# Attention values product turned round: probabilities as weights, values and ones as the moving side

## The reference, cut to what matters

```
Q = x @ wq (+ bq);  K = c @ wk (+ bk);  V = c @ wv (+ bv)      # c is x or the context
scores = Q K^T / sqrt(dk);  scores = where(mask == 0, -big, scores)
A = softmax(scores, axis=-1)
out = A @ V, heads side by side;   out @ wo (+ bo)
```

## Time and profile before

| | |
|---|---|
| median of 3 executions | 726.18 us (725.76 to 728.63) |
| profiled execution, its own time | 727.51 us |
| profiled execution, span from first to last instruction | 725.6 us |
| busy: PE / PE weight loads / DVE / ACT / POOL | 659.6 / 468.9 / 509.8 / 455.5 / 319.8 us |
| mean granted TensorE clock | 0.956 of full |

### The profile page before, as it was taken

How to read it: one execution, slowest core, us unless ns; L and a number is a source line. 1 busy time by engine, 2 the same in 40 slices (tenths; PEclk the granted TensorE clock), 3 DMA queues, 4 the chain that set the end, 5 groups by cost and what they waited for, 6 DMA issues and landing times.

```text
span 725.6 us, 26905 instructions
## 1 busy us (share of the span) xinstructions
PE 659.6 (91%) x9470; PEld 468.9 (65%) x9470; DVE 509.8 (70%) x1259; ACT 455.5 (63%) x1274; POOL 319.8 (44%) x540
## 2 busy tenths in 40 slices
PE   1999999999999999999999779899946989999995
PEld 1566666777777766666666537899933656666773
DVE  0598999888887778888888633344413689988784
ACT  1467677777777787777777442355513567777874
POOL 2244544466667653333477661245532254543110
PEclk9999999999999999999999669999975899999998
DMA  8333434332333321111111001122232011111110
GB/s 265 92 100 91 95 94 95 75 71 66 97 90 112 89 69 34 44 36 42 37 53 39 25 32 45 31 65 68 64 108 70 23 35 43 35 29 33 48 41 27
DMA packets 60047, 47.32 MB, mean 65 GB/s; under 512 B 7833, under 2 KB 54429, under 8 KB 58800
## 3 DMA queue, kind: packets, MB, share of 16 engines
q1 hardware_dynamic: 53152, 28.57, 14.2%
q10 hardware_dynamic: 4528, 13.25, 7.4%
q0 software_dynamic: 2272, 4.24, 1.8%
HBM read 25.41 MB, written 14.79 MB: 55 GB/s over the span
## 4 chain that ended last, share of the span: by engine, by line
PE 68%; issue 15%; POOL 7%; DVE 4%; ACT 2%; DMA 2%; ACTq 1%; SPq 0%; POOLq 0%; DVEq 0%
PE ps L569 11%; PE ps L606 9%; PE ps L792 5%; PE ps L730 5%; PE ps L803 5%; PE ps L655 4%; PE ps L643 4%; PE ps L672 4%; PE ps L738 4%; POOL k_by_j L499 3%; PE ps L711 3%; PE ps L758 2%; PE ps L656 2%; PE ps L591 2%; PE ps L683 2%
## 5 line engine op out<-in xcount | busy, mean ns | idle before, releaser
L1098 DVE TENSOR_REDUCE top<-ps 128x16 f32<-128x1024 f32 (+1 forms) x96 | 108.9, 1134 | 38.7 <-PE ps L569 37.0
L499 POOL TENSOR_TENSOR k_by_j<-k_t,cst 128x512 f32<-128x512 f32 (+1 forms) x96 | 95.6, 996 | 81.4 <-ACT k_t L907 45.0
L491 POOL TENSOR_TENSOR rstd<-spread,half_neg 128x1 f32<-128x1 f32 x80 | 44.6, 557 | 193.2 <-DVE spread L1191 115.0
L569 PE MATMUL ps<-k_by_j,q_t 32*64 32x256 f32 (+1 forms) x1536 | 123.8, 392 | 1.2
L606 PE MATMUL ps<-cst,prob 128*128 128x128 f32 x704 | 119.7, 291 | 1.7 <-ACT prob L928 1.5
L606 PEld LDWEIGHTS ps<-cst,prob 128*128 128x128 f32 x704 | 76.8, 143 | 61.5 <-issue 45.2
L1057 DVE RECIPROCAL inv<-ps 128x128 f32<-128x128 f32 x96 | 91.8, 956 | 32.9 <-PE ps L738 30.6
L928 ACT ACTIVATE prob<-prob 128x1024 f32<-128x1024 f32 (+1 forms) x96 | 94.8, 988 | 22.8 <-DVE prob L1114 22.5
L1114 DVE TENSOR_TENSOR prob<-ps,top 128x1024 f32<-128x1024 f32 (+1 forms) x96 | 108.3, 1128 | 0.7
L877 ACT ACTIVATE prob_t<-ps 128x512 f32<-128x512 f32 (+1 forms) x96 | 53.9, 561 | 38.0 <-PE ps L606 37.5
L865 ACT ACTIVATE prob_t<-ps 128x512 f32<-128x512 f32 (+1 forms) x96 | 53.9, 561 | 28.5 <-PE ps L606 27.4
(11 more groups left out here) (155 smaller groups left out, 1213.4 us busy)
## 6 DMA issues: line engine op xcount, KB each, us to landing
sorted_rows<-zero_rows ACTq DMA_DIRECT2D x32, 276.2 KB, 2.7
stage_m<-in_m SPq DMA_DIRECT2D x80, 64.0 KB, 2.0
stage_x<-x_t SPq DMA_DIRECT2D x80, 64.0 KB, 1.9
mow<-in_mow SPq DMA_DIRECT2D x18, 256.0 KB, 3.1
stage_kv<-in_ctx_t SPq DMA_DIRECT2D x64, 64.0 KB
rows_in<-sorted_rows SPq DMA_DIRECT2D x39, 65.0 KB, 1.8
wat<-in_wat ACTq DMA_DIRECT2D x1, 1280.0 KB, 7.6
stage_x<-in_x_t SPq DMA_DIRECT2D x16, 64.0 KB, 2.0
```

What stands on the lines that cost most here:

```text
L499: pool.tensor_tensor(k_by_j[:, p, 0:nj, :], k_t[:, p:p + 1, :].broadcast_to([128, nj, TOK]), cst[:, cj:cj + nj].unsqueeze(2).broadcast_to( ...
L569: mm = pe.matmul(ps[S * b:S * b + S, 2 * p + bank, r * nj * S:(r + 1) * nj * S].rearrange("p (h k) -> p h k", k=S), q_t[rows_g, p, S * b:S ...
L1098: dve.tensor_reduce(top[:, p, 0:nh].rearrange("p (b h) -> p b h", b=2), sc, AX.X, ALU.max).then_inc(top_d, 1)
```

## The change

The values product is turned round. The transposed probabilities (128 rows, 64 queries as columns) are now the stationary weights, and the values are the moving side. The moving side has, for a pair of heads, the values of both heads and two columns that are one on the rows of the even or the odd head: 18 columns for heads of 8 features, 34 for heads of 16. So the product gives values and sums at once, and the eight matmuls (L738) with ones as weights are gone. There are no zero columns any more, and nothing is accumulated. The result has tokens on the partitions, `heads_q`; DVE takes the reciprocal of 16 (or 8) sums a token instead of 128, and multiplies with a broadcast. Because the output projection needs features on the partitions, PE transposes `heads_q` (new, in the slot ahead of the transpose of the normalised rows), and ACT copies that from PSUM into `heads_t` (new, between the copy of the second half of the probabilities and the copy into `x_t`). The output projection waits for this copy (`ht_e`) instead of for DVE. ACT copies the values in two instructions a pair instead of four in the phases with 16 heads. GpSimd writes the two columns of ones once, at the start.

```
-        v_16 = sb("v_16", [128, 2, 2, 8, 32])
-        v_8 = sb("v_8", [128, 2, 2, 4, 32])
+        v_16 = sb("v_16", [128, 2, 2, 8, 18])
+        v_8 = sb("v_8", [128, 2, 2, 4, 34])
-        inv = sb("inv", [128, 2, D])
+        inv = sb("inv", [128, 2, 16])
+        heads_q = sb("heads_q", [128, 2, D])
...
+        def heads_at(pair):
+            nh = heads(pair)
+            w = 2 * D // nh + 2
+            at_ = ps[:, B_HEADS, 0:nh // 2 * w].rearrange("p (q c) -> p q c", c=w)
+            return at_[:, :, 0:w - 2], at_[:, :, w - 2:w]
...
@@ pool, once @@
+            for vb, w in ((v_16, 18), (v_8, 34)):
+                q = vb.shape[3]
+                pool.tensor_copy(vb[:, :, :, :, w - 2:w].rearrange("p a b q c -> p (a b q) c"),
+                                 cst[:, C_HALF:C_HALF + 2].unsqueeze(1).broadcast_to([128, 4 * q, 2])).then_inc(set_ones, 1)
...
@@ pe, slot, ahead of the transpose of the normalised rows @@
+                pr = at(OFF_OUT)
+                if pr is not None:
+                    wait_pair(pe, heads_d, pr)
+                    pe.transpose(ps[:, B_HEADS, HT], heads_q[:, pr.p, :], ident).then_inc(ht_d, 1)
...
@@ pe, output projection @@
-                    wait_pair(pe, heads_d, pr)
+                    wait_pair(pe, ht_e, pr)
...
@@ pe, values product @@
-                    wait_pair(pe, heads_d, pr, 1)
+                    wait_pair(pe, ht_e, pr, 1)
...
-                    for b in range(2):
-                        for k in range(step):
-                            for g in range(4):
-                                q = g * step + k
-                                half, c = divmod(q, npr // 2)
-                                mm = pe.matmul(ps[32 * g:32 * g + 32, B_HEADS, S * b:S * b + S],
-                                               vb[:, p, b, q, :],
-                                               prob_t[:, p, half, c * 128 + S * b:c * 128 + S * b + S],
-                                               start=k == 0, stop=k == step - 1, skip_group_check=True)
-                    for k in range(step):
-                        for g in range(4):
-                            half, c = divmod(g * step + k, npr // 2)
-                            mm = pe.matmul(ps[32 * g:32 * g + 32, B_HEADS, 128:128 + TOK], own_ones(pr, k),
-                                           prob_t[:, p, half, c * 128:c * 128 + TOK],
-                                           start=k == 0, stop=k == step - 1, skip_group_check=True)
+                    for q in range(npr):
+                        half, c = divmod(q, npr // 2)
+                        for b in range(2):
+                            mm = pe.matmul(ps[S * b:S * b + S, B_HEADS, w * q:w * q + w],
+                                           prob_t[:, p, half, c * 128 + S * b:c * 128 + S * b + S],
+                                           vb[:, p, b, q, :], start=True, stop=True, skip_group_check=True)
...
@@ act, slot, between the copy of pt1 and the copy into x_t @@
+                pr = at(OFF_OUT)
+                if pr is not None:
+                    wait_pair(act, ht_d, pr)
+                    wait_pair(act, out_d, pr, 2)
+                    act.activation(heads_t[:, pr.p, :], ps[:, B_HEADS, HT], ACT.Copy).then_inc(ht_e, 1)
...
@@ dve, first in the slot @@
-                    dve.reciprocal(inv[:, p, :], ps[:, B_HEADS, 128:128 + TOK]).then_inc(inv_d, 1)
-                    wait_pair(dve, out_d, pr, 2)
+                    nh = heads(pr)
+                    values, total = heads_at(pr)
+                    dve.reciprocal(inv[:, p, 0:nh].rearrange("p (q c) -> p q c", c=2), total).then_inc(inv_d, 1)
+                    wait_pair(dve, ht_d, pr, 2)
                     wait_pair(dve, inv_d, pr)
-                    dve.tensor_tensor(heads_t[:, p, :], ps[:, B_HEADS, 0:TOK], inv[:, p, :], ALU.mult)\
-                        .then_inc(heads_d, 1)
+                    dve.tensor_tensor(heads_q[:, p, :].rearrange("p (q c d) -> p q c d", c=2, d=D // nh),
+                                      values.rearrange("p q (c d) -> p q c d", c=2),
+                                      inv[:, p, 0:nh].rearrange("p (q c) -> p q c", c=2).unsqueeze(3)
+                                      .broadcast_to([128, nh // 2, 2, D // nh]), ALU.mult).then_inc(heads_d, 1)
```

More of the change, by code:

```diff
@@ L72 @@
 C_STEP, C_UPTO, C_BLOCK = 150, 166, 230
-C_O16 = C_BLOCK + JB
-C_O8, C_END = C_O16 + 64, C_O16 + 96
+C_HALF = C_BLOCK + JB
+C_END = C_HALF + 2
 OFF_PROJ, OFF_V, OFF_SCORE, OFF_PV, OFF_OUT, OFF_XT = 0, 1, 2, 3, 4, 5
@@ L240, in build @@
         XT, FB, OUT = (slice(128 * n, 128 * n + 128) for n in range(3))
+        HT = slice(256, 384)
         B_SH, B_SY = (0, 1), (2, 3)
@@ L246, in build @@
         loaded = {k: sem(f"loaded_{k}") for k in ("small", "x_tok", "rows", "wat", "ff", "l3", "order", "mo")}
-        set_zero, set_id, set_bv, set_order, set_mm, set_bias, set_rows = (
-            sem(k) for k in ("set_zero", "set_id", "set_bv", "set_order", "set_mm", "set_bias", "set_rows"))
+        set_zero, set_id, set_bv, set_order, set_mm, set_bias, set_rows, set_ones = (
+            sem(k) for k in ("set_zero", "set_id", "set_bv", "set_order", "set_mm", "set_bias", "set_rows", "set_ones"))
         ld_x = [sem(f"ld_x{p}") for p in range(2)]
@@ L251, in build @@
         ld_m = [sem(f"ld_m{p}") for p in range(2)]
-        proj_d, vproj_d, score_d, pt0_d, pt1_d, pv_d, out_d, xt_d = (
-            sem(k) for k in ("proj_d", "vproj_d", "score_d", "pt0_d", "pt1_d", "pv_d", "out_d", "xt_d"))
+        proj_d, vproj_d, score_d, pt0_d, pt1_d, pv_d, out_d, xt_d, ht_d, ht_e = (
+            sem(k) for k in ("proj_d", "vproj_d", "score_d", "pt0_d", "pt1_d", "pv_d", "out_d", "xt_d", "ht_d", "ht_e"))
         q_e, k_e, v_e, exp_d, pt0_e, pt1_e, xt_e = (
@@ L720, in slot @@
                     wait_pair(pe, v_e, pr)
[L721 removed]
+                    wait_pair(pe, ht_e, pr, 1)
                     wait_pair(pe, pt0_e, pr)
                     wait_pair(pe, pt1_e, pr)
[L724 to L740 removed]
+                    if isinstance(pr.n, int) and pr.n == 0:
+                        pe.wait_ge(set_ones, 2)
+                    w = 2 * D // heads(pr) + 2
+                    for q in range(npr):
[4 more added lines that the diff above has]
+                                           vb[:, p, b, q, :], start=True, stop=True, skip_group_check=True)
                     mm.then_inc(pv_d, 1)
@@ L936, in slot @@
                         rows_p = slice(S * par, S * par + S)
-                        src = ps[rows_p, B_PROJ, 256:384]
-                        if dk == 8:
-                            dst = v_16[rows_p, p, :, :, :].rearrange("r b (g k) c -> r (b g) (k c)", k=2)
-                            dst = dst.rearrange("r bg (k c) -> r bg k c", k=2)
-                            for k in range(2):
-                                ins = act.activation(
-                                    dst[:, :, k, 16 * k + 8 * par:16 * k + 8 * par + 8],
-                                    src.rearrange("r (bg k d) -> r bg k d", k=2, d=8)[:, :, k, :], ACT.Copy)
-                        else:
-                            ins = act.activation(
-                                v_8[rows_p, p, :, :, 16 * par:16 * par + 16].rearrange("r b q c -> r (b q) c"),
-                                src.rearrange("r (bq d) -> r bq d", d=16), ACT.Copy)
+                        vb = v_16 if dk == 8 else v_8
+                        ins = act.activation(vb[rows_p, p, :, :, dk * par:dk * par + dk].rearrange("r b q c -> r (b q) c"),
+                                             ps[rows_p, B_PROJ, 256:384].rearrange("r (bq d) -> r bq d", d=dk), ACT.Copy)
                     ins.then_inc(v_e, 1)
@@ L1305, in constants @@
     cst[:, C_IOTA:C_IOTA + E] = np.arange(E)
-    par, col = r[:, None] // S, np.arange(32)
-    for k in range(2):
-        cst[:, C_O16 + 32 * k:C_O16 + 32 * k + 32] = col // 8 == 2 * k + par
-    cst[:, C_O8:C_O8 + 32] = col // 16 == par
+    cst[:, C_HALF:C_HALF + 2] = r[:, None] // S == np.arange(2)
     cst[:, C_BASE:C_BASE + E] = NTOK * np.arange(E)
```

3 lines of the change are left out of this document (removed).

## The result

| | before | after |
|---|---|---|
| median, same chip | 726.55 us (725.76 to 728.63, 4 runs) | 768.32 us (760.74 to 769.58, 4 runs) |
| profiled execution | 727.5 us | 760.74 us |
| mean granted clock, profiled | 0.956 | 0.929 |

The changed kernel is slower: the ratio is 1.0545, interval 1.0484 to 1.0606. The forecast was 740 us with a range up to 751. The other executions of the changed kernel had mean clocks of 0.902 to 0.913, lower than the profiled one, so the profile shows a mild case of what follows.

A forecast was written before the change was run, and what follows sets the result against it. The prediction took a loop of PE and ACT through the copy into x_t to bound the 16-head slots. Terms 1.9 + 10.8 + 1.1 + 1.8 - 2.1 = +13.5 gave 741.0 profiled, 739.7 median, said as 740 us; range 730 to 751.

The forecast's parts named there:

- The clock: Rival: fewer streamed columns bring PE the lower clock; ten slots at half speed cost some 30 us, 770 us; chance 0.02.
- The product's piece: PE's values product with sums: 16 rounds of 0.055 plus 0.16, 1.04 us against 1.02; +1.9 us in all.
- two rivals about the load: PE's product: weights load faster, 0.61 a piece, 702 us, chance 0.09; loads not under streams, 1.25, 758 us, chance 0.07.
- the lower bound: PE's values product at half the forecast round, 0.028 us: a piece of 0.61 us, kept as not excluded.
- The copy on ACT: New copy on the PE-ACT loop delays x_t and output projection by 0.18 a slot; 60 slots, +10.8 us.
- The copy costs the loop nothing: Rival: the output projection's wait was not ACT's after all, so no change, 728 us; chance 0.08.
- Phase 3: PE's wait for DVE's rank absorbs the copy's 0.18; steady slots unchanged, six edge slots +1.1 us.
- Phase 5: ACT's copy has slack, so only the transpose counts: slot 3.93 to 4.06; with three drain slots +1.8 us.
- DVE: Reciprocal of 16 elements instead of 128 saves 67 us of DVE, counting only where PE waits behind it: -2.1 us.
- The edges: DVE's saving at the run's start, two slots from phase 4 into 5 (0.7 and 0.5), and last drain slots: -2.1 us.
- the 0.52 that PE waits there: PE's wait at the start of the run, taken to be behind DVE's reciprocal and so saved.
- The sum without the clock: Product 1.9, copy 10.8, phase 3 1.1, phase 5 1.8, DVE -2.1: +13.5 us, with no clock effect.

The follow-up runs named there:

- experiments 1: Changed kernel, each values-product matmul streaming 64 columns instead of 18 (34 in phase 5), filler and should-be-zero parts at 0.37: 739.45 us, ratio 1.0165.
- experiment 5: Changed kernel with 64 streamed columns in each values-product matmul, filler and should-be-zero parts zero, so the output is the reference's: 740.06 us, ratio 1.0158.
- experiment 6: Changed kernel with 32 streamed columns in the 16-head phases (the needed 34 in phase 5), zero filler: 752.8 us, ratio 1.0365.
- 7: Changed kernel with 64 streamed columns and zero filler in phase 0 only, 18 and 34 in later phases: 765.38 us, ratio 1.0539.
- Experiment 4: Kernel before, its sums' matmuls streaming 16 columns instead of 128, so sums are of 16 tokens only: 718.01 us, ratio 0.9862.
- Experiments 2: Changed kernel with the new copy into heads_t moved from ACT to DVE, behind its top reduction: 755.86 us, ratio 1.0361.
- 3: Changed kernel with 64 streamed columns (filler 0.37) and the copy into heads_t on DVE: 732.21 us, ratio 1.0059.
- experiment 9: Changed kernel with 64 columns, transposes and ACT copies into heads_t and x_t moved ahead of the probabilities' second half: 727.35 us, ratio 0.9995.
- experiment 10: Kernel before with the transpose and copy into x_t moved ahead of the probabilities' second half: 722.15 us, ratio 0.9918.

## Why the prediction was wrong, and where it was right

Its direction was right, its size was not: 740 forecast, 768 measured.

- **The step that failed** is the rival "The clock". The sum of the forecast puts the clock at nothing, and the rival got a chance of 0.02 with the words "It was 1.00 in the stretch of phase 0". That row is a steady stretch that stands at 2.4 GHz in both kernels. The places that decide were not read: where the clock first rises (33 to 34 us in the kernel before), the end of phase 3 and the start of phase 4, near both of which PEclk of the kernel before already shows digits of 6 and 5. There the changed kernel stays at 1.2 GHz, or falls to it, where the kernel before does not. The change took the columns streamed by product and sums of a slot from 16 x 64 and 8 x 128 down to 16 x 18, while their time stayed at 1.04 (1.02 before). What the clock took is 23.2 of the 33.3 us of the profiled execution. The rival's mechanism (fewer columns, lower clock) was the right one. Its price, ten slots at 3 us, was near: eight slots at 2.9. That its 770 stands so close to the 768 measured is in part luck, since executions of one and the same kernel went from 754.87 to 770.0 us. That the width is the cause is shown by experiments 1 and 5 (same records, 740), with clocks of 0.957 to 0.963 in all 27 executions with 64 columns throughout and 0.901 to 0.930 in all with 18; by the dose of 6 (753); and by 7, where phases 3 and 4 have the layout of 5 but 18 columns, and lose. Experiment 4 agrees from the other side, weakly. More columns read and more results written go together in these runs; which of the two counts was not separated.
- **The product's piece:** 1.04 forecast, 1.04 measured. The two rivals about the load (0.61 and 1.25) fall, and the lower bound with them: with a 64-column weight load a round takes 0.059 in a steady slot, whether 18 or 64 columns follow. The forecast had rounds of 0.055 and a fixed part of 0.16; measured are 0.059 and some 0.10, two small errors that cancel.
- **The copy on ACT:** 0.18 a slot forecast; slots grew by 0.19 or 0.20 in phases 0 (5.30 to 5.49), 1 (7.39 to 7.58) and 2 (5.21 to 5.40), the product's 0.02 among it, so the copy cost 0.17. Experiments 2 and 3 take that away again. "The copy costs the loop nothing" falls.
- **Phase 3:** "unchanged" at the upper level; 6.20 became 6.23. **Phase 5:** 0.13 more forecast, 3.92 to 4.04 measured.
- **DVE:** the reciprocal gave back 96 x (956 - 248) ns = 68 us, as said (67). The engine's busy time fell by only 48.5 (509.8 to 461.3); 13.3 of the missing 19.5 are `normed`, which takes longer now, below. The edges gave less than the 2.1 forecast: where phase 4 passes into phase 5, two slots fell by 0.24 each, 0.5 instead of 1.2, and the last slots rose (3.75 to 3.94, 3.17 to 3.33). And the earlier trace rows was misread: the 0.52 that PE waits there ends with ACT's exponential, and DVE stands only behind that.
- **The sum without the clock:** +10.1 outside the nine slots, +13.5 forecast. 58 slots of phases 0, 1, 2 and 4 make +9.2 of it, 0.16 on average instead of 0.20, and phase 3 outside its three slots gave 0.5 back where 1.1 was to be lost. Experiments 1 and 5, at 739.5 and 740.1, look like the forecast of 740 with the clock as it was, but carry some 3 us of their own for the filler (0.04 in each of some 80 slots): without it the change is worth +11, and the exact hit is luck.

What stays open: what exactly the chip measures when it grants the level, and why the place varies between executions. The runs order three widths; they give no threshold, and I name none. The Trainium skill, TensorE: Matmul & The Clock Gate, "The mechanism", states that a load overlaps matmuls in flight only when the row group differs. The trace of experiment 5 disagrees: every record of its product uses all 128 rows, and a round of a 64-column load and a 64-column stream takes 0.059 us, where the two in series would take 0.107. With the earlier trace rows and L643 that is two cases against the rule.

## What to carry to other kernels

Where the weight load sets a matmul's time, as here, thinning the moving side saves nothing and can cost the clock; filler up to the load's own length cost 0.04 us in a piece of 1.04 here and was worth 24 to 28 us (740.06 against 763.97 and 768.32). When a change takes columns out of a stream, read the granted clock and the durations where the engine starts, drains and starts again, not in the steady stretch. And a copy added between two engines that wait for each other costs about its start-to-start time (0.17 here) in every slot, however idle its engine is in sum. Taking the copies off that loop was worth 12.7 us in the changed kernel with filler (experiment 9, 740.06 to 727.35) and 5.8 us in the kernel before, which has one of them (experiment 10, 727.9 to 722.15).

## What the runs showed that was not expected

- TensorE busy 24.00 of 24.00 us and yet at 1.2 GHz for nearly all of it (window 391 to 415 of the kernel after, clock 0.53): an engine that the profile shows as full was not enough for the upper level here. For some 200 records with 64 columns the window of experiment 5 shows 1.00.
- At the start of a run the clock in the windows reads 1.00, although the scores matmul takes 1.13 us there and not 0.66. The trace has no clock entry before the first rise (50.9 us in the kernel after), and a stretch without one counts as full. So the level has to be read from durations in that place, and the mean clocks given above leave the start out: experiment 6 shows 0.959 with a start at half speed. The window of the kernel after, with the stretch in which its values product took 1.90 us:

```profile
30.00:50.00 20.00, 20.00 (x164) 13.56 (x164) 12.35 (x22) 7.91 (x18) 5.57 (x5) 1.00 0.27 76
```
- `normed` on DVE, same operation and shape in both kernels, has two durations. The groups by line of the kernel before and of the kernel after:

```profile
L1069 DVE TENSOR_SCALAR normed<-y,moments,rstd 128x128 f32<-128x128 f32 x48 | 18.5, 386 | 0.0
```

```profile
L1074 DVE TENSOR_SCALAR normed<-y,moments,rstd 128x128 f32<-128x128 f32 x48 | 31.8, 663 | 0.4 <-POOL rstd L499 0.2
```

Its mean goes from 386 to 663 ns, 13.3 us in all, off the chain in the steady slots. The timeline of the kernel after, in phase 0, shows what it stands beside:

```profile
118.61 1.04 POOL L507 TENSOR_TENSOR k_by_j<-k_t,cst 128x512 f32<-128x512 f32 x1
...
118.80 0.93 DVE L1074 TENSOR_SCALAR normed<-y,moments,rstd 128x128 f32<-128x128 f32 x1
```

POOL's instruction ends at 119.65 and `normed` at 119.73. In both kernels every `normed` of 0.39 us or more ends 0.08 to 0.09 us behind an instruction of POOL that had begun before it, and those without such an overlap take 0.34 to 0.35. In the kernel before, `normed` starts later in POOL's instruction and waits for less of it (0.40 us in the same phase). So the trace shows DVE's instruction held until POOL's ends; no run moved one of the two to prove it.
